# Attention parts of three, three and two key chunks instead of two, with seven score slots written ahead

## The reference

```
h = relu(conv(embedding[x]))                     # 2 taps, 32 groups
a = layernorm(h)
q, k, v = heads of a Wq^T, a Wk^T, a Wv^T        # 8 heads of 64
h = h + softmax(q k^T / 8) v  Wo^T + a
n = layernorm(h)
xa = (layernorm(n) * ln_g + ln_b) attn_w^T + attn_b + n
y = gelu(xa fc1[e]^T + b1[e]) fc2[e]^T + b2[e]   # expert e: the tokens of its own eighth
h = h + gelu(y next_w^T + next_b)
```

## Time and profile before

| | us |
|---|---|
| median of 3 runs (408.17 to 408.68) | 408.19 |
| the profiled execution | 409.11 |
| its span | 407.2 |
| PE busy | 395.0 (97%) |
| PE weight loads busy | 238.1 (58%) |
| POOL busy | 292.7 (72%) |
| ACT busy | 254.7 (63%) |
| DVE busy | 224.5 (55%) |

### The profile page before, as it was taken

One profiled execution on the slowest core, in us unless ns is written; L12 is line 12 of the kernel. 1 busy time (PEld: TensorE's weight loads), 2 busy tenths in 40 slices (PEclk: granted clock), 3 DMA queues, 4 the chain that ended last, 5 costly groups with the idle time before them and its releaser, 6 DMA issues.

```text
span 407.2 us, 6494 instructions
## 1 busy us (share of the span) xinstructions
PE 395.0 (97%) x2518; PEld 238.1 (58%) x2518; DVE 224.5 (55%) x304; ACT 254.7 (63%) x347; POOL 292.7 (72%) x145
## 2 busy tenths in 40 slices
PE   8898999999999999999999999999999989999996
PEld 8765554454555445544645555464558535489995
DVE  1798765565656555656665565657563700564322
ACT  1556566676667575767676575858573596436763
POOL 3062088969899989999998999899989487900011
PEclk9999999999999999999999999999999999999999
DMA  7000101011220121012103222240125014000001
GB/s 247 2 1 0 54 0 54 6 47 26 82 52 2 54 54 52 3 54 54 52 2 105 48 110 54 54 150 7 57 52 157 0 55 155 2 1 14 15 26 53
DMA packets 28507, 20.49 MB, mean 50 GB/s; under 512 B 21276, under 2 KB 23708, under 8 KB 28476
## 3 DMA queue, kind: packets, MB, share of 16 engines
q1 hardware_dynamic: 27900, 19.09, 17.3%
q10 hardware_dynamic: 576, 0.98, 0.7%
HBM read 18.77 MB, written 1.17 MB: 49 GB/s over the span
## 4 chain that ended last, share of the span: by engine, by line
PE 88%; DVE 4%; ACT 2%; DMA 2%; SPq 1%; issue 1%; POOL 0%; ACTq 0%; POOLq 0%
PE acc_o L583 27%; PE slot L571 24%; PE slot L509 9%; PE slot L497 6%; PE slot L518 4%; PE acc_o L639 4%; PE slot L628 4%; PE acc_o L476 2%; PE acc_o L436 2%; DVE half_maxes L961 2%; PE slot L594 2%; DMA max_plane<-rows_scratch 1%; SPq L386 1%; PE slot L451 1%; PE slot L534 1%; PE acc_o L451 1%
## 5 line engine op out<-in xcount | busy, mean ns | idle before, releaser
L961 DVE TENSOR_REDUCE half_maxes<-slot 128x2 f32<-128x1024 f32 x128 | 156.3, 1225 | 98.1 <-PE slot L509 97.9
L761 ACT ACTIVATE probs<-slot 128x1024 f32<-128x1024 f32 x128 | 124.7, 1024 | 82.2 <-PE slot L571 82.2
L583 PE MATMUL acc_o<-probs,v_all 128*64 128x512 f32 x512 | 123.7, 604 | 0.0
L1160 POOL TENSOR_TENSOR sums<-sums,probs 128x1024 f32<-128x1024 f32 x31 | 74.0, 2387 | 2.4 <-ACT probs L761 2.3
L1160 POOL TENSOR_TENSOR odd_sum<-odd_sum,probs 128x1024 f32<-128x1024 f32 x31 | 74.5, 2404 | 0.0
L1160 POOL TENSOR_TENSOR sums<-probs 128x1024 f32<-128x1024 f32 x16 | 37.9, 2368 | 44.0 <-ACT probs L761 44.0
L583 PEld LDWEIGHTS acc_o<-probs,v_all 128*64 128x64 f32 x512 | 31.2, 136 | 59.0 <-issue 39.7
L509 PE MATMUL slot<-k_round,q_round 64*128 64x512 f32 x256 | 56.9, 447 | 1.6 <-DVE half_maxes L961 1.3
L509 PEld LDWEIGHTS slot<-k_round,q_round 64*128 64x128 f32 x256 | 23.6, 183 | 57.0 <-issue 46.3
L571 PE MATMUL slot<-q_round,k_round 64*128 64x512 f32 x256 | 51.8, 400 | 1.7 <-ACT slot L819 0.8
L571 PE MATMUL slot<-q_round,k_rest 64*128 64x512 f32 x256 | 50.6, 390 | 0.0
(11 more groups left out here) (114 smaller groups left out, 423.1 us busy)
## 6 DMA issues: line engine op xcount, KB each, us to landing
max_plane<-rows_scratch SPq DMA_DIRECT2D x16, 512.0 KB, 3.6
inv_sb<-inv_scratch SPq DMA_DIRECT2D x14, 256.0 KB, 3.9
max_rows_of<-maxes SPq DMA_DIRECT2D x128, 0.5 KB, 2.0
v_all<-in_fc SPq DMA_DIRECT2D x4, 512.0 KB, 5.9
fc_late<-in_fc SPq DMA_DIRECT2D x4, 512.0 KB, 5.6
residual<-in_x SPq DMA_DIRECT2D x2, 512.0 KB, 5.9
out_h<-probs SPq DMA_DIRECT2D x8, 128.0 KB, 1.8
v_all<-in_w ACTq DMA_DIRECT2D x3, 256.0 KB, 7.4
```

The costliest lines, as they stand in the source:

```text
L583: last = pe.matmul(acc_o[head_rows(h), cols], v_all[:, s, kc, head_rows(h)], probs[unit(s, kc, half) % TILES][:, h, :], start=(kc == 0), s ...
L761: act.activation(probs[u % TILES][:, :, :].rearrange("p h n -> p (h n)"), slot[:, :], ACT.Exp, scale=SCALE).then_inc(exped, 1)
L961: dve.reduce_max(half_maxes[:, :, qc, keys], slot[:, :].rearrange("p (h n) -> p h n", h=2), AX.X).then_inc(maxed, 1)
L1160: pool.tensor_tensor(chain[:, :, :], first[:, :, :], probs[kc][:, :, :], ALU.add).then_inc(own, 1)
```

## The change

A half's eight units now go in parts of three, three and two, so a step has six parts instead of eight. In a part of three the order is max, exp, exp, max, exp, max, the beside items, the fills of the next part, and the values of the part before. The key chunks whose slots are written ahead become 3, 4, 6 and 7 instead of 2, 4 and 6, save chunk 4 in the first half: seven of sixteen in a step instead of six. With the exceptions of the first and last steps this is 53 units instead of 44. The beside items of step 7 move to the new part numbers, and with two fills in a part both are written one behind the other.

```diff
--- before.py
+++ after.py
@@ -43,7 +43,9 @@
 BANK = 512
 SLOTS = 3
 UNITS = 2 * KCH
-PARTS = KCH
+PARTS_OF_HALF = ((0, 1, 2), (3, 4, 5), (6, 7))
+HALF_PARTS = len(PARTS_OF_HALF)
+PARTS = 2 * HALF_PARTS
 TILES = KCH
 CONV_BANK = (0, 1, 6, 7)
 
@@ -68,16 +70,22 @@
 EXP_TABLE_BEHIND = ("max", *MAXES[6])
 
 
-FFN_ITEMS = {(STEPS - 1, 0): [("wo",)], (STEPS - 1, 3): [("nt",)], (STEPS - 1, 5): [("xa",)], (STEPS - 1, 6): [("last den", 0)]}
-
-
-PREFILLED = (2, 4, 6)
-UNFILLED = ((0, 2, 0), (STEPS - 1, 4, 0), (STEPS - 1, 4, 1))
+FFN_ITEMS = {(STEPS - 1, 0): [("wo",)], (STEPS - 1, 3): [("nt",)], (STEPS - 1, 4): [("xa",)], (STEPS - 1, 5): [("last den", 0)]}
+
+
+PREFILLED = (3, 4, 6, 7)
+UNFILLED = ((0, 3, 0), (STEPS - 1, 3, 1), (STEPS - 1, 4, 1)) + tuple((s, 4, 0) for s in range(STEPS))
 
 
 def units_of(s, part):
 
-    return [(s, 2 * (part % 4) + i, part // 4) for i in range(2)]
+    return [(s, kc, part // HALF_PARTS) for kc in PARTS_OF_HALF[part % HALF_PARTS]]
+
+
+def maxes_of(s, part):
+
+    first = AHEAD + s * UNITS + sum(len(units_of(s, p)) for p in range(part))
+    return [("max", *m) for m in MAXES[first:first + len(units_of(s, part))]]
 
 
 def beside_values(s, part):
@@ -85,28 +93,29 @@
     items = []
     if part == 0 and s + 1 < STEPS:
         items += [("k", s + 1), ("q", s + 1)]
-    if part == 3 and s > 0:
+    if part == 2 and s > 0:
         items.append(("den", s - 1))
     return items + FFN_ITEMS.get((s, part), [])
 
 
 def part_items(s, part):
 
-    maxes = [("max", *m) for m in MAXES[AHEAD + 2 * (s * PARTS + part):][:2]]
-    items = maxes[:1]
-    items += [("exp", *u) for u in units_of(s, part)] + maxes[1:]
+    maxes, exps = maxes_of(s, part), [("exp", *u) for u in units_of(s, part)]
+    items = maxes[:1] + exps[:2] + maxes[1:2]
+    for e, m in zip(exps[2:], maxes[2:] or [None] * len(exps[2:])):
+        items += [e, m] if m else [e]
     beside = beside_values(s, part)
     items += beside
-    if part % 4 < 3:
-        items.append(("fill", *units_of(s, part + 1)[0]))
+    if part % HALF_PARTS + 1 < HALF_PARTS:
+        items += [("fill", *u) for u in units_of(s, part + 1)]
     if s > 0 or part > 0:
         items += [("pv", *u) for u in units_of(*divmod(s * PARTS + part - 1, PARTS))]
     if part == 0 and s > 0:
         items.append(("o", s - 1, 1))
-    if part == 4:
+    if part == HALF_PARTS:
         items += [("o", s, 0)] * (s + 1 < STEPS) + [("inv", s - 1)] * (s > 0)
     if s == STEPS - 1 and part in (1, 2, 3):
-        items.append(("norms", part))
+        items += [("norms", part)]
     return items
```

## The result

| | us |
|---|---|
| before, median of 4 runs (408.17 to 408.68) | 408.33 |
| after, median of 4 runs (413.47 to 414.8) | 414.0 |
| after / before, 95% interval | 1.0139, 1.0121 to 1.0158 |
| after, the profiled execution and its span | 413.47, 411.7 |

The account below looks back on a forecast made before the run. PE was taken as the bound, with POOL close behind. Steps 1 to 6 (+5.4), step 0 (-0.2) and step 7 and behind (+0.6) sum to +5.8 us, taking the median 408.19 to 414.0; 8-in-10 range 410.0 to 417.0.

Parts of the forecast that it names:

- (a): Third exp item of a part waits for the first's exponential: 0.24 us, in three parts a step, 0.72.
- (b): Second max of a half's last part waits for the first max's DVE pass: 0.19 us, twice a step, 0.38.
- (c): Second part of half 1: two writes queue on ACT, delaying chunk 4 by 0.18 and chunk 5 by 0.56; 0.74 us.
- step 0: First step: 0.95 saved, 1.60 of new waits, 0.82 gained as the wait for the maxima plane goes; -0.2 us.
- step 7 and behind: Last step and after: -1.18 work, +0.24 (a), +1.2 "xa", +0.5 "last den", -0.2 for a write's wait; +0.6 us.
- The price of a burst: Entering and leaving the value matmuls on PE costs 0.36 us; two fewer plus one pair (0.23) save 0.95 a step.
- nt: Step 7 item of eight transposes, waiting for ACT behind eight normalisations; its wait of 1.11 us stays about the same.
- xa: Step 7 item, due at 5.75 us after "nt" starts, waits for an exponential ending at 6.92: 1.2, or 0.9 with slack.
- last den: End of step 7: its first item comes after the last exponentials and DVE's sum of 2.78, costing about +0.5 us.
- Work alone: Rival: PE takes up releases without restarts, so only fewer bursts, pairs and the plane's wait count: 8.7 us faster, 399.5; 10%.
- No change: Rival: the ACT queue of (c) doesn't form and (b) is covered, so waits are 0.95 a step: 408.2 to 410; 4%.
- The heavier case: Rival: ACT writes don't overlap and waits chain, up to 2.4 us of waits a step: 417 to 418.5; 12%.

Follow-up runs that it names:

- e5: Kernel before with both passes shortened (exponential 512 of 1024 columns from the ninth unit on, maximum 256 of each 512): 404.44 us.
- e6: Changed kernel with both passes shortened (exponential 512 of 1024 columns from the ninth unit on, maximum 256 of each 512): 396.26 us.
- e7: Changed kernel with only the maximum shortened, to 256 of each 512 columns: 410.3 us.
- e1: Changed kernel with only chunks 3 and 6 written ahead, four slots of sixteen: 411.18 us.
- e3: Changed kernel, but chunk 7 is not written ahead in either half: 413.01 us.
- e2: Changed kernel, but chunk 4 of the second half is not written ahead: 412.51 us.
- e11: Kernel before, with chunk 0 of the second half written ahead in steps 1 to 7 and four max items in step 0's fifth part: 406.74 us.
- e4: Kernel before, parts of two, with chunk 7 written ahead too, eight slots of sixteen: 408.09 us.
- e9: Kernel before, with fourteen max items ahead of step 0 instead of twelve: 409.2 us.
- e12: As e11, with chunk 7 written ahead too in both halves: 406.98 us.
- e8: Changed kernel with only the exponential shortened, to 512 of 1024 columns from the ninth unit on: 404.43 us.

## Why the prediction was right

The forecast of 414.0 was met, by its own mechanism. That it was met to the tenth is luck: the sum had +5.8 us, the medians moved by 5.67 from a median that is 0.14 higher with the fourth run, and the stretches of the two profiles move by 5.25. The terms were read apart:

| term | predicted | measured |
|---|---|---|
| work saved a step | -0.95 | -0.94 (e5 against e6) |
| (a), three times | 0.72 | 0.74 (198.38 for 198.13, and two more of 0.25 and 0.24) |
| (b), twice | 0.38 | 0.41 (231.34 for 231.13; "den" at 212.98 for 212.78) |
| (c) | 0.18 + 0.56 | 0.16 + 0.51 |
| a step | +0.9 | +0.87 |
| step 0 | -0.2 | -0.25 |
| step 7 and behind | +0.6 | +0.22 |

- **The price of a burst**. The burst of three units in PE's timeline:

```profile
207.93 2.79 PE L592 MATMUL acc_o<-probs,v_all 128*64 128x512 f32 x12
210.66 0.50 PE L518 MATMUL slot<-k_round,q_round 64*128 64x512 f32 x2
```

2.73 - 1.87 = 0.86 for the third unit, the same as in the earlier trace rows. Both came from rows of before.

- **(c) and two writes in a row.** No row of before showed them; I took 0.96 from one to the next. Two took 1.98, a pitch of 0.95, and the copy followed at once. Of the cases left open none chained further.

- **The sum of a step.** The terms of the table add up to +0.88, the step shows +0.87. The waits alone can be told from the short passes too: 1.94 in after less 0.13 in before is 1.81, and (a) to (c) measure 1.82. But one of the two (b) is not the wait that I named: in the last part of the first half the 0.20 is held by DVE's maximum and by the exponential that "den" needs, and e7, where the maximum is early, keeps it.

- **Step 0.** The plane's wait of 1.02 is gone. In the timeline of ACT and PE of after, the writes stand in line, and the second one makes the same wait as in every other step:

```profile
67.24 1.97 ACT L828 ACTIVATE slot<-max_plane 128x1024 f32<-128x1024 f32 x2
...
68.98 0.40 PE L580 MATMUL slot<-q_round,k_rest 64*128 64x512 f32 x2
...
69.27 0.51 PE L580 MATMUL slot<-q_round,k_round 64*128 64x512 f32 x2
```

- **Step 7: the step of the sum that was mis-sized.** In PE's timeline "nt" and "xa" read:

```profile
341.05 1.09 PE L534 MATMUL slot<-ident,normed 128*128 128x128 f32 x8 [1.51 <-ACT probs L770]
...
347.95 1.13 PE L543 MATMUL slot<-normT,small 128*128 128x512 f32 x2 [0.97 <-ACT probs L770]
```

"xa" waits 0.97, inside the 0.9 to 1.2, of which the sum had taken 1.2. "nt" waits 1.51 and not 1.11, where I had "about the same": it waits for the first exponential behind the same eight normalisations, and PE, with less work ahead, stands there 0.4 sooner. And "last den" did not wait at all, for which I had +0.5. POOL, DVE and PE at the end of step 7:

```profile
357.41 2.35 POOL L1175 TENSOR_TENSOR sums<-sums,odd_sum 128x1024 f32<-128x1024 f32 x1
...
361.08 1.22 DVE L999 TENSOR_TENSOR sums<-probs 128x1024 f32<-128x1024 f32 x1
...
361.26 2.05 PE L637 MATMUL slot<-xaT,v_all 128*128 128x128 f32 x16
...
363.24 1.94 PE L616 MATMUL slot<-sums,ones 128*64 128x512 f32 x8
...
365.11 3.06 PE L527 MATMUL slot<-woT,attn_out 128*128 128x128 f32 x25
```

PE goes from the hidden layer to "last den" at 363.24 without a gap, because DVE's sum had taken 1.22 us and not the 2.78 of before. POOL's last sum had ended at 359.76. Before, it ran beside DVE's, in POOL's timeline:

```profile
353.79 2.36 POOL L1166 TENSOR_TENSOR sums<-sums,odd_sum 128x1024 f32<-128x1024 f32 x1
```

So three terms were off: "nt" by +0.4, "last den" by -0.5, "xa" by -0.2. With them +0.6 becomes about +0.2 (-1.18 + 0.24 + 0.97 + 0.4 - 0.2), and +0.22 was measured. The -1.18, the 0.24 and the -0.2 in it were not read apart. All of it is too small to move the result.

- **The rivals.** Work alone (399.5) fell with e1 to e3 and needs e6's short passes to come true. No change would need (c) away and (b) covered; e2 shows that without chunk 4 three quarters of the loss stay (4.3 of 5.7 us). The heavier case would need writes without overlap; they overlap. POOL had idle time left.

## What to carry to other kernels

When one engine has no gaps, count what a new order saves, but then walk each shared buffer: from the last instruction that fills it, through its releaser's pass, to the second instruction that needs it, and count what stands between. Here three slots in turn carry about 1.6 us of other work, and a release takes 1.85. A saving pays only where nobody waits for it: the same kind of write was worth 0.25 a step in a place with room (e11), and cost 0.20 behind another write (chunk 4, e2).

## What the runs showed of the hardware

- **DVE's sum of two SBUF tiles of 128 x 1024 takes 2.75 to 2.78 us beside a sum on POOL and 1.21 to 1.22 without one.** It was the longer one in the seven profiles with parts of two units (before, e4, e5, e9 to e12), where POOL's last sum had started 0.7 us ahead of it, and the shorter one in the seven with parts of three (after, at 361.08, e1 to e3, e6 to e8), where POOL was done. The timeline of POOL and DVE in e11:

```profile
351.69 2.36 POOL L1175 TENSOR_TENSOR sums<-sums,odd_sum 128x1024 f32<-128x1024 f32 x1
...
352.38 2.75 DVE L999 TENSOR_TENSOR sums<-probs 128x1024 f32<-128x1024 f32 x1 [0.57 <-ACT probs L770]
```

POOL ends at 354.05, DVE at 355.13, 1.08 later; alone it needs 1.22. So, by this estimate, in the 1.67 us beside POOL it got through a tenth of its work, while POOL's own sum takes 2.35 to 2.37 either way. No run changed this alone: the order of the whole step differs between the two groups. The Trainium skill (GPSIMD Engine Reference, 1. Specifications) says that GpSimd shares its access to SBUF with VectorE and that instructions of VectorE with two inputs in SBUF contend with it. The trace agrees, and shows that the price is nearly a full stop. DVE's maximum, which reads PSUM, takes 1.23 in a stretch with POOL busy for 45.61 of 48 us.

- **Waits for different engines hide one another**: 0.64 us of 1.94 a step (e7, e8 and e6) goes only when both releases come early, so such losses can't be added up from single experiments.
- **A restart costs more than the wait.** In every case above the second pair follows the first in 0.33 to 0.34 and not in 0.23; of (a)'s 0.25, 0.11 are that.
